# Stack loads by token halves, the first norm's rows on ScalarE, and a convolution in two parts, in a hybrid convolution-attention-experts kernel

## The reference, cut to what matters

```python
# layer 0: per-image norm, three projections with a 3x3 depthwise convolution, attention between channels
xn = (x - mu) * rsqrt(var + EPS) * ln_g + ln_b
Q, K, V = (_proj(xn, wp, bp, wd, bd) for each kind)        # 8 heads of 24 channels
attn = softmax(einsum('bhnc,bhnd->bhcd', K, Q) / alpha)    # 24 x 24 per head
x = w_f @ (V attn) + b_f + xn
# layer 1, on t = tokens of x (1024 x 192)
h = (t - mean(t)) / sqrt(var(t) + 1e-5)                    # the "first norm", per token over 192 channels
wei = softmax(causal(q @ k.T) * 32 ** -0.5)                # 6 heads of 32, causal over the 1024 tokens
t = t + W_proj(W_proj(wei @ v) + b) + b
t = t + sum over the 2 best of 4 experts of gate * expert(norm(t))
```

## Time and profile before

| | us |
|---|---|
| median of 3 runs | 4002.49 (3996.62, 4002.49, 4022.53) |
| the profiled execution | 3976.27 |
| its span | 3974.5 |
| PE busy | 3252.2 (82%) |
| DVE busy | 2360.8 (59%) |
| ACT busy | 1836.1 (46%) |
| POOL busy | 1076.2 (27%) |

### The profile page before, as it was taken

One profiled execution on the slowest core, in us unless ns is written; L12 is line 12 of the kernel. 1 busy time (PEld: TensorE's weight loads), 2 busy tenths in 40 slices (PEclk: granted clock), 3 DMA queues, 4 the chain that ended last, 5 costly groups with the idle time before them and its releaser, 6 DMA issues. The chain is left out here.

```text
span 3974.5 us, 72989 instructions
## 1 busy us (share of the span) xinstructions
PE 3252.2 (82%) x26642; PEld 2468.7 (62%) x26642; DVE 2360.8 (59%) x5963; ACT 1836.1 (46%) x3868; POOL 1076.2 (27%) x1542
## 2 busy tenths in 40 slices
PE   3687887878779787787978779787499999999995
PEld 1465565565545555565565556555488888888884
DVE  3466565666647566465666647566456565656664
ACT  0345263543625435263543526445355555555553
POOL 1011202112020211202112020211336555565543
PEclk9898898988889898898988879897799999999998
DMA  6344353443533335343443533334123433333332
GB/s 148 97 102 122 96 136 89 101 107 87 145 106 94 97 93 132 96 123 92 102 107 88 147 101 94 93 97 116 46 71 106 118 99 109 99 114 94 117 104 86
DMA packets 213097, 414.47 MB, mean 104 GB/s; under 512 B 66799, under 2 KB 130223, under 8 KB 211673
## 3 DMA queue, kind: packets, MB, share of 16 engines
q1 hardware_dynamic: 188169, 359.44, 34.3%
q0 software_dynamic: 24576, 50.36, 4.2%
HBM read 242.86 MB, written 117.71 MB: 91 GB/s over the span
## 5 line engine op out<-in xcount | busy, mean ns | idle before, releaser
L971 DVE TENSOR_REDUCE minus_max<-ps 128x1 f32<-128x128 f32 (+7 forms) x768 | 575.9, 750 | 514.8 <-PE ps L1649 510.0
L1647 PE MATMUL ps<-KS,QS 96*128 96x512 f32 (+3 forms) x1152 | 433.0, 430 | 295.8 <-DMA KS<-QKl 260.1
L1386 ACT ACTIVATE p_sb<-ps,minus_max 128x128 f32<-128x128 f32 (+7 forms) x768 | 567.7, 741 | 115.5 <-DVE minus_max L971 112.0
L1659 PE MATMUL ps<-ident,p_sb 128*128 128x128 f32 x3456 | 555.2, 286 | 31.1 <-ACT p_sb L1386 7.8
L1401 ACT ACTIVATE PT<-ps 128x512 f32<-128x512 f32 (+3 forms) x640 | 340.6, 532 | 395.4 <-PE ps L1659 388.6
L1273 DVE TENSOR_TENSOR g_lo<-g,g_hi 128x512 fp32r<-128x512 f32 x402 | 315.4, 786 | 348.5 <-ACT g_hi L1476 296.9
L1475 ACT ACTIVATE g<-ps,bcur 128x512 f32<-128x512 f32 x402 | 276.6, 688 | 474.3 <-PE ps L1837 373.0
L1853 PE MATMUL ps<-w_all,g_hi 128*128 x1608 | 442.1, 355 | 18.2 <-ACT g_hi L1476 9.2
L706 POOL COPY inverse_wide<-inverse_sums 128x192 f32<-128x192 f32 x128 | 44.7, 349 | 1484.5 <-DVE inverse_sums L993 1484.5
L1647 PEld LDWEIGHTS ps<-KS,QS 96*128 96x128 f32 x1152 | 217.6, 212 | 357.1 <-DMA KS<-QKl 265.7
L1659 PEld LDWEIGHTS ps<-ident,p_sb 128*128 128x128 f32 x3456 | 385.1, 146 | 79.3 <-issue 33.3
(11 more groups left out here) (277 smaller groups left out, 5924.4 us busy)
## 6 DMA issues: line engine op xcount, KB each, us to landing
ring<-padded_scratch SPq DMA_DIRECT2D x576, 204.0 KB
routed_rows<-zero_rows SPq DMA_DIRECT2D x67, 384.0 KB, 6.9
xgt<-routed_rows SPq DMA_DIRECT2D x67, 384.0 KB
expert_rows<-y_rows SPq DMA_DIRECT2D x67, 384.0 KB, 2.5
QS<-QKh SPq DMA_DIRECT2D x64, 256.0 KB, 4.6
KS<-QKh SPq DMA_DIRECT2D x64, 256.0 KB, 5.0
padded_scratch<-xpad SPq DMA_DIRECT2D x16, 870.0 KB, 4.6
x_sb<-x SPq DMA_DIRECT2D x16, 768.0 KB, 7.6
```

What stands on the lines that cost most here:

```text
L971: v.tensor_reduce(nmx[:, qc, h:h + 1], score_place(n), AX, ALU.max, negate=True).then_inc(mx_sb, 1)
L1386: a.activation(p_sb[n % NP][:, 0:P * (qc + 1)], score_place(n), ACT.Exp, bias=nmx[:, qc, h:h + 1], accum_out=ls[:, qc, h:h + 1]).then_inc( ...
L1647: t.matmul(o[:, k0:k0 + keys], QS[0:96, h, P * qc:P * (qc + 1)], KS[0:96, h, k0:k0 + keys], start=True, stop=k0 + keys < P * (qc + 1), ski ...
L1659: last = t.transpose(bank(pass_bank(piece))[:, P * k:P * (k + 1)], p_sb[n % NP][:, P * (k0 + k):P * (k0 + k + 1)], ident[:, :])
```

## The change

- SP loads the stacks in two token halves. `QK_ORDER` now makes all three groups of token half 0 first (`QK_FIRST` = 3). The first 12 DMAs (heads 0 and 1, half 0) wait for the first block and for all transposes of `xhat`; then come 6 for the keys and 6 for the queries of heads 2 to 5, half 0, and last 12 for all heads, half 1. These are 36 DMAs in place of 24, of 64, 128 and 192 KB, with rows of 2 KB where there were rows of 4 KB. Units with `qc` below 4 need half 0 alone, in the scores and for the places of `PT`; the others wait for two new semaphores.
- `normed` moves from DVE to ACT, as scale and bias of an activation. For this DVE writes minus the mean (one instruction more per four blocks), and POOL multiplies it by the inverse deviation (one more instruction behind the power). On ACT both halves of `normed` stand ahead of `high_channels(0)`. PE waits for single token blocks in `norm_transposes`.
- Round 5 of the convolutions is done in two halves: the first where it stood, the second behind `channel_products(1)`. Its copy on ACT is two instructions.
- POOL sends 12 rows' DMAs ahead of `token_rstd` and 4 behind it, where it was 8 and 8.

```diff
...
@@ -421,9 +421,9 @@
-        QK_ORDER = [(0, 0), (1, 0), (0, 1), (2, 0), (1, 1), (2, 1)]
+        QK_ORDER = [(0, 0), (1, 0), (2, 0), (0, 1), (1, 1), (2, 1)]
...
-        QK_FIRST = 1
+        QK_FIRST = PAIR_GROUPS
...
@@ -527,29 +527,36 @@
-                def load_queries(j, first, end, signal):
...
+                def load_queries(j, first, end, half, signal):
+                    cols = slice(BANK * half, BANK * (half + 1))
                     for r, part in enumerate((QKh, QKl, QKh)):
-                        sp.dma_start(QS[D * r:D * (r + 1), 2 * first + j:2 * end:2, :].bitcast(F32),
-                                      part[D * j:D * (j + 1), first:end, :].bitcast(F32)).then_inc(signal, 16)
...
+                        sp.dma_start(QS[D * r:D * (r + 1), 2 * first + j:2 * end:2, cols].bitcast(F32),
+                                      part[D * j:D * (j + 1), first:end, cols].bitcast(F32)).then_inc(signal, 16)
...
-                sp.wait_ge(qk_lo, NQ * i + QK_ORDER.index((0, 1)) + 1)
...
+                sp.wait_ge(qk_lo, NQ * i + 1)
+                sp.wait_ge(lnT_ps, 4 * (i + 1))
                 for j in range(2):
-                    load_queries(j, 0, 1, stack_ld[j])
-                    load_keys(j, 0, 1, stack_ld[j])
-                sp.wait_ge(qk_lo, NQ * (i + 1))
+                    load_queries(j, 0, 1, 0, stack_ld[j])
+                    load_keys(j, 0, 1, 0, stack_ld[j])
+                sp.wait_ge(qk_lo, NQ * i + PAIR_GROUPS)
+                for j in range(2):
+                    load_keys(j, 1, PAIR_GROUPS, 0, stack_ld[2 + j])
                 if i:
 
                     sp.wait_ge(sent, SENT * i)
                 for j in range(2):
-                    load_queries(j, 1, PAIR_GROUPS, stack_ld[2 + j])
-                    load_keys(j, 1, PAIR_GROUPS, stack_ld[2 + j])
+                    load_queries(j, 1, PAIR_GROUPS, 0, stack_ld[2 + j])
+                sp.wait_ge(qk_lo, NQ * (i + 1))
+                for j in range(2):
+                    load_queries(j, 0, PAIR_GROUPS, 1, stack_ld[4 + j])
+                    load_keys(j, 0, PAIR_GROUPS, 1, stack_ld[4 + j])
                 if i + 1 < B:
                     load_image(sp, i + 1)
...
@@ -691,7 +698,9 @@
-                g.tensor_tensor(rstd[:, 1, ch], rstd[:, 0, ch], minus_half[:, 0:TPC], ALU.pow).then_inc(rstd_sb, 1)
+                g.tensor_tensor(rstd[:, 1, ch], rstd[:, 0, ch], minus_half[:, 0:TPC], ALU.pow).then_inc(rstd_pw, 1)
+                pool.wait_ge(rstd_pw, 2 * i + j + 1)
+                g.tensor_tensor(rstd[:, 3, ch], rstd[:, 2, ch], rstd[:, 1, ch], ALU.mult).then_inc(rstd_sb, 1)
...
@@ -722,11 +731,11 @@
                 if i:
-                    send(i - 1, 0, TPC)
+                    send(i - 1, 0, 6)
                 token_rstd(i, 0)
                 token_rstd(i, 1)
                 if i:
-                    send(i - 1, TPC, NC)
+                    send(i - 1, 6, NC)
...
@@ -932,16 +940,9 @@
+                    if mv is tmv:
+                        v.tensor_scalar(rstd[:, 2, ch], mv[:, ch, 0], -1.0, None, ALU.mult)
                     v.tensor_scalar(veps_of[:, 0, ch], mv[:, ch, 1], 1e-5, None, ALU.add).then_inc(signal, 1)
-
-            def normed(i, j):
-
-                dve.wait_ge(rstd_sb, 2 * i + j + 1)
...
@@ -980,7 +981,10 @@
                         elif h == 1:
-                            for signal in stack_ld:
+                            for signal in stack_ld[0:4]:
+                                dve.wait_ge(signal, STACK_LOADS * (i + 1))
+                        if qc == TPC and h == 0:
+                            for signal in stack_ld[4:6]:
                                 dve.wait_ge(signal, STACK_LOADS * (i + 1))
...
@@ -1197,11 +1201,8 @@
                         token_stats(i, k - 1, y_sb, k, tmv, rstd, veps)
-                    if k == TPC + 2:
-                        normed(i, 0)
                 token_stats(i, NC - 1, y_sb, NC, tmv, rstd, veps)
                 low_channels(i, 0)
-                normed(i, 1)
                 for n in range(QK_FIRST):
                     low_qk(i, n)
                 low_channels(i, 1)
...
@@ -1351,6 +1352,13 @@
+            def last_values_out(i, nh):
+                act.wait_ge(conv_ps, QC * (NR * i + NR - 1) + nh + 1)
+                ins = a.activation(vp[:, 1, BANK * nh:BANK * (nh + 1)], bank(2 + nh), ACT.Identity,
+                                   bias=convb[:, PAIRS + 1:PAIRS + 2])
+                if nh:
+                    ins.then_inc(conv_sb, 1)
...
@@ -1368,6 +1376,14 @@
+            def normed(i, j):
+                act.wait_ge(rstd_sb, 2 * i + j + 1)
+                for k in range(TPC * j, TPC * (j + 1)):
+                    scale, bias = rstd[:, 1, k:k + 1], rstd[:, 3, k:k + 1]
+                    a.activation(xhat[:, k, 0:C], t_sb[:, k, 0:C], ACT.Identity, bias=bias, scale=scale)
+                    a.activation(xhat[:, k, C:2 * P], t_sb[:, k, P:C], ACT.Identity, bias=bias, scale=scale
+                                 ).then_inc(xhat_sb, 1)
...
@@ -1420,11 +1436,14 @@
                 conv_qk(i, 2)
+                last_values_out(i, 0)
                 mixing(i, 0)
-                conv_out(i, 5)
                 conv_qk(i, 3)
                 channel_exp(i, 1)
+                last_values_out(i, 1)
                 mixing(i, 1)
+                for j in range(2):
+                    normed(i, j)
                 high_channels(i, 0)
...
@@ -1587,12 +1606,13 @@
-                pe.wait_ge(xhat_sb, NC * i + TPC * (j + 1))
...
+                    pe.wait_ge(xhat_sb, NC * i + TPC * j + kk + 1)
...
@@ -1637,8 +1657,10 @@
-                if n < H:
+                if qc == 0:
                     pe.wait_ge(stack_ld[h if h < 2 else 2 + h % 2], STACK_LOADS * (i + 1))
+                if qc == TPC and h < 2:
+                    pe.wait_ge(stack_ld[4 + h], STACK_LOADS * (i + 1))
...
@@ -1731,10 +1753,11 @@
-                conv(i, 5)
+                conv(i, 5, [0])
                 mixing(i, 0)
                 conv_transposes(i, 3)
                 channel_products(i, 1)
+                conv(i, 5, [1])
                 pe.wait_ge(mix_sb, 2 * i + 1)
...
```

More of the change, by code:

```diff
@@ L273, in hybrid_block_kernel @@
             "veps2 xhat2_sb gsub rowsum_sb count_sb slot_sb table_sb")
-        xstat, img_veps, xg_sb, xn_sb, xn_flat, wide_sb, rstd_sb, rstd2_sb, tb_sb, img_rstd = sems(
-            "xstat img_veps xg_sb xn_sb xn_flat wide_sb rstd_sb rstd2_sb tb_sb img_rstd")
+        xstat, img_veps, xg_sb, xn_sb, xn_flat, wide_sb, rstd_pw, rstd_sb, rstd2_sb, tb_sb, img_rstd = sems(
+            "xstat img_veps xg_sb xn_sb xn_flat wide_sb rstd_pw rstd_sb rstd2_sb tb_sb img_rstd")
         ring_ld = [sem(f"ring_ld{p}") for p in range(PAIRS)]
-        stack_ld = [sem(f"stack_ld{n}") for n in range(4)]
+        stack_ld = [sem(f"stack_ld{n}") for n in range(6)]
         x_ld, scr_w, t_st, sent, cleared, dram_written = sems("x_ld scr_w t_st sent cleared dram_written")
@@ L740, in _ @@
                 token_rstd2(i, 1)
-            send(B - 1, 0, TPC)
-            send(B - 1, TPC, NC)
+            send(B - 1, 0, NC)
             pool.wait_ge(w_split, 1)
@@ L934, in token_stats @@
                     ch = slice(k - TPC + 1, k + 1)
+                    if mv is tmv:
+                        v.tensor_scalar(rstd[:, 2, ch], mv[:, ch, 0], -1.0, None, ALU.mult)
                     v.tensor_scalar(veps_of[:, 0, ch], mv[:, ch, 1], 1e-5, None, ALU.add).then_inc(signal, 1)
-            def normed(i, j):
-                dve.wait_ge(rstd_sb, 2 * i + j + 1)
-                for k in range(TPC * j, TPC * (j + 1)):
-                    v.tensor_scalar(xhat[:, k, 0:C], t_sb[:, k, 0:C], tmv[:, k, 0:1], rstd[:, 1, k:k + 1],
-                                    ALU.subtract, ALU.mult)
-                    v.tensor_scalar(xhat[:, k, C:2 * P], t_sb[:, k, P:C], tmv[:, k, 0:1], rstd[:, 1, k:k + 1],
-                                    ALU.subtract, ALU.mult).then_inc(xhat_sb, 1)
             def low_channels(i, j):
@@ L1511, in _, with conv @@
             pe.wait_ge(img_veps, 1)
-            def conv(i, r):
+            def conv(i, r, halves=range(QC)):
                 kind, n = ROUNDS[r]
@@ L1524, in conv @@
                     pe.wait_ge(exp_sb, NU * (i - 1) + NU - 1 + r)
-                for nh in range(QC):
+                for nh in halves:
                     for s in range(2):
@@ L1532, in conv @@
                                             start=s == 0, stop=s == 1, skip_group_check=True)
-                last.then_inc(conv_ps, 1)
+                    last.then_inc(conv_ps, 1)
             def conv_transposes(i, p):
@@ L1589, in norm_transposes @@
             def norm_transposes(i, j):
-                pe.wait_ge(xhat_sb, NC * i + TPC * (j + 1))
-                for b, c0 in ((4 + 2 * j, 0), (5 + 2 * j, P)):
-                    for kk in range(TPC):
+                for kk in range(TPC):
+                    pe.wait_ge(xhat_sb, NC * i + TPC * j + kk + 1)
```

(4 more changed lines are left out.)

13 lines of the change are left out of this document (7 added, 6 removed).

## The result

| | before | changed |
|---|---|---|
| median | 4001.7 us (4 runs, 3996.6 to 4022.5) | 4061.6 us (4 runs, 4055.0 to 4070.9) |
| profiled execution's span | 3974.5 | 4058.7 |
| of it, the image loop (last round of image 1 to that of image 16) | 2539.3 | 2594.8 |
| of it, behind the last score (experts) | 1178.1 | 1205.6 |

The ratio is 1.0146, 95% interval 1.0119 to 1.0173: the kernel became slower by 60 us, where I forecast no change (4009 us). The loop explains it: 55.5 us, 3.7 an image. Another 27.5 us between the two profiled executions lie in the experts' stage, which the change doesn't touch; a later profile of the unchanged kernel (before_again) has 1206.7 us there, so the first profile of before was a short one in that stage.

The account below looks back on a forecast made before the run. Stack loads were taken as bound by transfer, the loop behind them by DVE. −0.1 + 2.3 − 1.8 + 0.3 = +0.7 us for each of 15 images (+10), less 3 for the last, gave +7: 4009 us, range 3935 to 4062.

Parts of the forecast that it names:

- What bounds it, and the stacks: Stack loads in the image loop: bound by transfer at 223 GB/s; first units gain 6.4 us, next image's load lands later.
- T0: Issue of an image's first stack load; forecast to shift by −0.1 us, from +0.8 (norm on ACT) and −0.9 (convolution).
- R1: Faster rival: transfers don't bound the loads behind half 0, the image's load lands at T0' + 28.6; 3958 us, chance 0.17.
- R3: Slower rival: lower PE clock through all three first blocks and the transposes; 4063 us, chance 0.18 shared with a slow load rate.
- The convolution: Last round in two parts: products end 1.8 us sooner; between 0 and 1.9 us comes through, half taken, −0.9 an image.
- POOL: Four more sends ahead of the first power: it keeps its time within a microsecond, the second power decides; nothing counted.
- R4: Slower rival: the sends on POOL delay the power by more than 3 us; about 4050 us, chance 0.03.
- The catch-up and the lower clock: Behind DVE's wait: PE and ACT run ahead, DVE regains idle time, −1.8 us; PE's lower clock costs +0.3 an image.
- the wait: DVE at the next image's statistics stands until its load lands at T0' + 32.0, formerly passing at T0 + 29.7: +2.3 us.
- The last image: It loads no next image, so it keeps about half of the first units' 6.4 us gain: −3 us.
- R2: Faster rival: T0 comes earlier, first block at full clock, loads at 252 GB/s; 3952 us, chance 0.11.
- The likeliest case: The forecast itself for the whole kernel: no change, within 1%, own range 3975 to 4045 us, chance 0.51.

Follow-up runs that it names:

- conv_only: The kernel before with only the last values' convolution round done in two parts; 3816.4 us, ratio 0.9815.
- warm: The changed kernel with 56 idle matmuls an image on TensorE, ahead of the ninth unit's transposes while DVE waits; 3971.8 us, ratio 1.0217.

## Why the prediction was right or wrong

**What bounds it, and the stacks: right.** The next image's load, behind the longer queue, holds DVE. I had it at T0 + 32.0, and it is at 32.5 (39.9 to 72.4). In the seventh image half 0 had landed at T0 + 17.6 (17.9 forecast) and half 1 at 29.1 (28.5). The first units came 6.7 us earlier against T0, I had 6.4. The issue of 36 loads took 25.6 us and not 23, which the bytes behind it hid. With rows of 2 KB half 1 moved at 207 GB/s (2.36 MB in 11.4 us), a little under the 223 that I took. The Trainium skill's ceiling of 435 GB/s ("DMA: Bandwidth & Descriptors", "Specifications") would have made half 1 a matter of its issue, with the load landed as R1 has it, at T0 + 28.6 or before; the trace does not agree.

**T0: right in sum (+0.3 for −0.1), wrong in its parts.** That the sum came out is luck: its errors cancel. Eight activations took 3.1 us, not 2.0, the multiply 0.20, not 0.35. The way from the first block to T0 took 6.7 and not 5.8: the lower clock lasted longer than the one block that I gave it (see R3). The convolution gave 2.3 at the heads' end (26.8 to 24.5), not 0.9, and on the other kind of chip 4.7. For POOL I counted nothing, since I saw the second power as the one that decides. On the chip of the forecast that was right within 0.2 us. It is wrong on the other kind, where the heads end 5 us earlier: there the last send ends 4.6 us behind the variance and holds both powers, which is rival R4's mechanism, to which I gave 0.03.

**The catch-up and the lower clock: the step that failed.** I took −1.8 for idle time that DVE would get back and +0.3 for the clock, −1.5 together. Measured from the statistics to unit 23 the changed kernel is 1.5 us longer (19.1 for 17.55): the restart is 1.1 us closer to the statistics (1.49 for 2.60), and the stretch behind it 2.6 longer. The miss of 3.0 us an image, 45 us in all, is the largest part of the 53 us by which 4009 was short. Smaller ones are T0 (0.4 an image), the wait (2.7 for 2.3) and the last image (below); against them stands 1.0 us that the changed kernel gains behind unit 23 (82.9 to 81.9 us to the next image's round), for which I had no term. My error was in what the wait does to PE: I let PE "run ahead", but it was done with three units in 2 us, then idle for 8.7 and granted half of the clock, with the first output projection and wider scores to do. Before, the same low clock lay under the first, narrow units. The row that I took the 1.8 us from could have told me: beside DVE's 7.18 of 9.00 us it has PE busy for 8.34. I read these windows as ones where the loop runs on DVE, but PE, the busier of the two in both, had 0.66 us to give back in the first, not 1.8.

**The last image** gave 0.9 us (146.6 to 145.7 from its last round to its last scores), not 3.

**The rivals.** R3 gave 4063, and 4061.6 came, but that is mostly luck, since its price needs T0 at +3.5 and T0 moved by +0.3. Its mechanism came in part. The first block ran at the lower clock in all images, and in 9 of 16 the second took 2.0 us or more. The eighth image shows it; these rows of PE start the first block, the second and the third:

```profile
1358.28 0.79 PE L1629 MATMUL ps<-T_hi,wqkv_a_hi 128*128 128x512 f32 x1 [4.32 <-DVE T L953]
...
1360.58 0.63 PE L1629 MATMUL ps<-T_hi,wqkv_a_hi 128*128 128x512 f32 x1
...
1362.71 0.63 PE L1629 MATMUL ps<-T_hi,wqkv_a_hi 128*128 128x512 f32 x1
```

That is 2.30 us for the first and 2.13 for the second; the third took 1.50. In the seventh image it was 2.30, 1.44 and 1.16, and in the mean of images 2 to 15 2.30, 1.90 and 1.44. That is 5.6 us for the three, 1.1 more than the 2.3 + 2.26 of my sum. R1 is refuted by the load's landing at T0 + 32.5, where it needs 28.6, and R2 by the first block, 2.30 us in every image. The whole range held the time, but by 0.4 us (4061.6 in 3935 to 4062), which is luck too. The likeliest case, within 1% and 3975 to 4045, did not hold it.

## What to carry to other kernels

A load that starts earlier is no gain if what stands behind it in the same queue is needed first: ask of each transfer in the queue who waits for it next, and put the one with the nearest reader ahead. Here that one move was worth 4% in each of two pairs on the same chip. And price a wait of an engine by what TensorE does in it: idle time of 9 us was followed by 2.5 us more for the same work at the lower clock, and work put into such a gap can be worth more than the gap (conv_only: 2.9 us of idle time, T0 5.2 us earlier). Such work must fit the gap: the idle matmuls of warm ran over and lost what the clock gave back.

## What the runs showed of the hardware that was not expected

- Two kinds of chip. On the first and that of the second group, before the second softmax DVE (L911) starts up to 6.5 us late, put down to "remote", 55.2 us in 11 waits in before_again, and in the kernels with the round in two parts ACT's copy of the last values up to 5.5 us; in conv_only's profile there is no such wait. The kernel before differs by 2.7% between them (4000 and 3893 us). What it is stays open; no run here took it apart. It changes what an edit is worth. The changed kernel was never timed on the other kind. An estimate from warm (1.0217, of which some 1 us an image is warm's own) puts its ratio there at 1.018.
- How the 91 us of the norm's move divide between the order on ScalarE, the sends and the activations was not taken apart on that kind of chip. On the other, the order moved the first block by 2.0 us, and the sends held the first power for 4.6; twelve sends against eight were not tried alone.
